# Graph attention kernel, first layer: wide matmuls for even blocks, h recomputed, x1 written late, adjacency stored in 8 KB pieces

## The reference, cut to what matters

```python
h = relu(layernorm(x))
# layer 0: attention
wh = h @ W;  e = wh @ a1 + (wh @ a2).T;  e = where(e > 0, e, 0.2 * e)
x1 = x + elu(softmax(where(adj > 0, e, -9e15)) @ wh)
# layer 1: cosine attention
h = relu(layernorm(x1))
Qn, Kn = cos_normalize(h @ Wq.T), cos_normalize(h @ Wk.T)
prop = softmax(where(adj > 0, Kn @ Qn.T, -9e15), axis=1) @ h
y = x1 + 0.5 * prop + 0.5 * h        # where a row has neighbours, else h
```

## Time and profile before

| | us |
|---|---|
| median of 3 runs (2190.71 to 2191.54) | 2190.98 |
| the profiled execution's own time | 2189.39 |
| its span, first to last instruction | 2187.6 |

### The profile page before, as it was taken

How to read it: one execution, slowest core, us unless ns; L and a number is a source line. 1 busy time by engine, 2 the same in 40 slices (tenths; PEclk the granted TensorE clock), 3 DMA queues, 4 the chain that set the end, 5 groups by cost and what they waited for, 6 DMA issues and landing times.

```text
span 2187.6 us, 63203 instructions
## 1 busy us (share of the span) xinstructions
PE 2142.1 (98%) x26185; PEld 1733.5 (79%) x26185; DVE 1963.5 (90%) x1686; ACT 1752.8 (80%) x1928; POOL 33.0 (2%) x43
## 2 busy tenths in 40 slices
PE   5999999999999979999999999999999999999998
PEld 5999999999999956777777777777777777777776
DVE  7999999999999858889888898898898898898987
ACT  6687778878788668888888888888888888888886
POOL 1000000000000030000000000000000000000000
PEclk9999999999999989999999999999999999999999
DMA  6899999999999916565565665665665666656653
GB/s 248 328 382 401 390 405 397 401 402 399 403 400 388 361 40 217 193 223 204 207 215 196 224 212 196 220 220 193 214 221 200 212 204 216 215 194 218 218 193 115
DMA packets 153732, 573.52 MB, mean 262 GB/s; under 512 B 9936, under 2 KB 10576, under 8 KB 153168
## 3 DMA queue, kind: packets, MB, share of 16 engines
q1 hardware_dynamic: 142176, 546.02, 68.3%
q10 hardware_dynamic: 11376, 24.91, 3.0%
HBM read 558.24 MB, written 12.65 MB: 261 GB/s over the span
## 4 chain that ended last, share of the span: by engine, by line
PE 95%; DVE 2%; ACT 1%; issue 1%; DMA 0%; POOL 0%; ACTq 0%; POOLq 0%; DVEq 0%
PE bank L1197 32%; PE bank L1245 30%; PE bank L1266 21%; PE bank L1261 10%; DVE hl_buf L726 1%; PE bank L1152 1%; PE bank L1172 0%; DVE hl_buf L714 0%; DMA ring<-adj 0%; ACT hl_buf L558 0%; ACT ring L619 0%; POOL hl_buf L401 0%; PE bank L1094 0%; PE bank L1134 0%; DMA q_buf<-x 0%
## 5 line engine op out<-in xcount | busy, mean ns | idle before, releaser
L619 ACT ACTIVATE ring<-bank,th_col 128x512 f32<-128x512 f32 x1024 | 647.1, 683 | 231.0 <-PE bank L1245 223.3
L988 DVE SCALAR_TENSOR_TENSOR ring<-ring 128x2048 f32<-128x2048 int32 x256 | 586.4, 2291 | 154.5 <-ACT ring L619 154.5
L1197 PE MATMUL bank<-v_buf,ring 128*128 128x129 f16 (+1 forms) x12288 | 711.9, 220 | 6.3 <-DVE ring L902 6.1
L1197 PEld LDWEIGHTS bank<-v_buf,ring 128*128 128x128 f16 x12288 | 707.8, 98 | 9.8 <-issue 8.9
L1245 PE MATMUL bank<-v_buf,q_buf 128*128 128x512 f16 x3072 | 706.4, 380 | 5.2 <-ACT ring L619 5.2
L1266 PE MATMUL bank<-u_buf,hl_buf 128*128 (+1 forms) x8192 | 704.3, 220 | 0.0
L1266 PEld LDWEIGHTS bank<-u_buf,hl_buf 128*128 128x128 f16 x8192 | 631.8, 98 | 55.9
L902 DVE SCALAR_TENSOR_TENSOR ring<-r_ring,th_word,ring 128x1024 f32<-128x1024 f32 x512 | 619.3, 1277 | 19.3 <-ACT ring L448 19.1
L993 DVE TENSOR_TENSOR hl_buf<-ring,hl_buf 128x2048 f16<-128x2048 f32 x256 | 584.5, 2284 | 0.0
L1261 PE MATMUL bank<-u_buf,hl_buf 128*128 (+1 forms) x2048 | 557.9, 272 | 0.5 <-DVE hl_buf L993 0.5
L448 ACT ACTIVATE ring<-ring 128x2048 f32<-128x2048 int32 x256 | 481.2, 1908 | 88.4 <-DMA ring<-adj 85.0
(11 more groups left out here) (138 smaller groups left out, 433.0 us busy)
## 6 DMA issues: line engine op xcount, KB each, us to landing
ring<-adj SPq DMA_DIRECT2D x512, 1024.0 KB, 5.6
r_ring<-a_rows SPq DMA_DIRECT2D x8, 512.0 KB, 7.0
x_dram<-q_buf ACTq DMA_DIRECT2D x8, 512.0 KB, 7.2
h_dram<-hl_buf ACTq DMA_DIRECT2D x8, 512.0 KB, 7.4
r_ring<-x_dram ACTq DMA_DIRECT2D x16, 256.0 KB, 4.2
r_ring<-h_dram ACTq DMA_DIRECT2D x16, 256.0 KB, 4.4
out<-r_ring ACTq DMA_DIRECT2D x16, 256.0 KB, 4.8
r_ring<-k_rows ACTq DMA_DIRECT2D x15, 256.0 KB, 4.1
```

Of the source, the lines that this page charges most:

```text
L619: ins = nc.scalar.activation(p_ring[:, k, (2 * hf + m) * IW:(2 * hf + m + 1) * IW], bank[:, 2 * hf + m, :], ACT.Exp, scale=q_scale[:, j:j ...
L988: V.scalar_tensor_tensor(p_ring[:, k, :], adj_ring[:, k, :], 0.0, p_ring[:, k, :], ALU.is_gt, ALU.mult).then_inc(s_m, 1)
L1197: ins = mm(acc0(par, it), weights0(k, ps)[:, it // 4, jj, f], v2[:, bass.ds((2 * j + us) * VW, D + 1)], start=False, stop=False, skip_grou ...
```

## The change

- **Even blocks of layer 0** take two matmuls instead of three: one of 259 columns (`WIDE`) over high and low values side by side, then low by high with 129. The slot has 40 matmuls instead of 48. The 8 sums take 4 banks a set instead of 3; the high-by-low sums of even blocks stand in columns of their own and are added on DVE: for the denominators by two copies, a sum and a reciprocal, for the features by four instructions in `negative` that add into `z_buf`.
- **The exponential** loses DVE's `min`. ACT now forms relu(-z) and then exp(-that), and `preset` (three instructions over 4 banks, 1552 elements a partition instead of 1032) moves from behind `quotient` to behind the exponential.
- **h**: the high part is written by ACT behind `normalised` instead of by DVE. h isn't written to DRAM; layer 1 forms it again from x1 in four ACT instructions a chunk (`residual_h`), for which `rstd` and `nbias` are kept for all tiles.
- **x1**: chunks 0, 4 and 7 are written by ACT as before, the others by SP behind the last loads of layer 0.
- **Banks**: the work between the layers uses other PSUM banks, and PE waits for the end of the added step ("low") of chunk 6 and chunk 7 where it waited for the quotient.
- `sizes` on ACT and its matmul move from chunk 1 to chunk 0.
- **Adjacency in DRAM**: for one load of layer 0 a partition's data is one piece of 8 KB; loads of layer 1 still take 4 KB pieces, now 8 KB apart.

```diff
 VW = D + 2
+WIDE = VW + D + 1
...
 EARLY = 4
+X1_EARLY = (0, 4, 7)
+X1_LATE = (1, 5, 2, 6, 3)
 FOLDS = (0, 16, 48, T)
 LN = ("diff", "total", "m2", "dsq", "between", "var", "rstd", "nbias")
-EPI0 = ("den", "neg", "elu", "x1", "stats") + LN + ("hi", "lo")
+EPI0 = ("densum", "den", "low", "elu", "x1", "stats") + LN + ("lo",)
...
         def acc0(par, it):
-            b, k = 3 * par + it // 3, it % 3
-            return bank[:, b, k * (D + 1):(k + 1) * (D + 1)]
-        def acc0_group(par, b):
-            n = min(3, IT0 - 3 * b)
-            return bank[:, 3 * par + b, 0:n * (D + 1)].rearrange("p (n c) -> p n c", n=n)
+            k = it % 2
+            return bank[:, 4 * par + it // 2, k * WIDE:k * WIDE + D + 1]
+        def acc0_wide(par, it):
+            return bank[:, 4 * par + it // 2, 0:WIDE]
+        def acc0_column(par, col):
+            return bank[:, 4 * par:4 * par + 4, col]
         def ht_bank(g):
-            return bank[:, 6 + g % 2, :].bitcast(F16)
+            return bank[:, 2 + g % 2, :].bitcast(F16)
         def qk_pair(g):
-            return 0 if g < EARLY else 2 * ((g - EARLY) % 2)
+            return 0 if g < EARLY else 4 * ((g - EARLY) % 2)
         def qk_banks(g):
             b = qk_pair(g)
             return bank[:, b:b + 2, :].rearrange("p b n -> p (b n)")
         def key_bank(i):
-            return bank[:, 4 if i == 0 else 6 if i == 1 else 4 + 2 * ((i - 1) % 2), :]
+            return bank[:, 7 if i == 0 else 6 if i == 1 else 4 + 2 * ((i - 1) % 2), :]
...
-            adj_lanes = adj.rearrange("b j p n -> p b j n")
+            adj_lanes = adj.rearrange("c j p b n -> p c j b n")
             def load0(c, j, k):
-                sp.dma_start(slot(k, I32).rearrange("p (b j n) -> p b j n", b=2, j=1),
-                             adj_lanes[:, bass.ds(2 * c, 2), bass.ds(j, 1), :]).then_inc(s_adj[k], 16)
+                sp.dma_start(slot(k, I32), adj[c, j].rearrange("p b n -> p (b n)")).then_inc(s_adj[k], 16)
             def load1(i, j, k):
-                sp.dma_start(adj_ring[:, k, :].rearrange("p (b j n) -> p b j n", b=1, j=2),
-                             adj_lanes[:, bass.ds(i, 1), bass.ds(2 * j, 2), :]).then_inc(s_adj[k], 16)
+                sp.dma_start(adj_ring[:, k, :].rearrange("p (j n) -> p j n", j=2),
+                             adj_lanes[:, i // 2, bass.ds(2 * j, 2), i % 2, :]).then_inc(s_adj[k], 16)
...
             chunks0(chunk)
+            for c in X1_LATE:
+                sp.wait_ge(s_ev, len(EPI0) * c + EPI0.index("x1") + 1)
+                sp.dma_start(x1_dram[:, c * C0:(c + 1) * C0], xs[:, c * C0:(c + 1) * C0]).then_inc(s_x1w[c % (NC0 // 2)], 16)
...
-                for i in range(3):
-                    g = acc0_group(par, i)
-                    ins = nc.scalar.activation(g, v_sum[:, :].unsqueeze(1).to_broadcast([P, g.shape[1], D + 1]),
+                sums = bank[:, 4 * par:4 * par + 4, 0:WIDE + D + 1]
+                nc.scalar.activation(sums[:, :, D + 1:WIDE].rearrange("p b (s n) -> p b s n", s=2),
+                                     ident[:, 0:D // 2 + 1].unsqueeze(1).unsqueeze(1).to_broadcast([P, 4, 2, D // 2 + 1]),
+                                     ACT.Copy, scale=0.0)
+                for k in range(2):
+                    ins = nc.scalar.activation(sums[:, :, k * WIDE:k * WIDE + D + 1],
+                                               v_sum[:, :].unsqueeze(1).to_broadcast([P, 4, D + 1]),
...
                     ins.then_inc(s_free, 1)
-                    if not (isinstance(c, int) and c == NC0 - 1):
-                        act.wait_ge(s_free, c + 1)
-                        act.nop(nofuse=True)
+                def exponential():
+                    act.wait_ge(s_ev, at("low"))
+                    nc.scalar.activation(e_buf, z_buf, ACT.Relu, scale=-1.0).then_inc(s_neg, 1)
+                    act.wait_ge(s_neg, c + 1)
+                    nc.scalar.activation(e_buf, e_buf, ACT.Exp, scale=-1.0).then_inc(s_ea, 1)
+                    if c != NC0 - 1:
                         preset(par)
-                def exponential():
-                    act.wait_ge(s_ev, at("neg"))
-                    nc.scalar.activation(e_buf, e_buf, ACT.Exp).then_inc(s_ea, 1)
                 def root():
-                    act.wait_ge(s_ev, at("x1"))
-                    act.dma_start(x1_dram[:, bass.ds(c * C0, C0)], xs[:, bass.ds(c * C0, C0)]).then_inc(s_x1w, 16)
+                    if c in X1_EARLY:
+                        act.wait_ge(s_ev, at("x1"))
+                        act.dma_start(x1_dram[:, bass.ds(c * C0, C0)], xs[:, bass.ds(c * C0, C0)]).then_inc(
+                            s_x1w[c % (NC0 // 2)], 16)
...
                         act.wait_ge(s_ev, at("nbias"))
-                        if not (isinstance(c, int) and c == 0):
-                            act.wait_ge(s_hw, 16 * c)
                     act.nop(nofuse=True)
                     for it in range(lo, hi):
                         ins = nc.scalar.activation(h_buf[:, it * P:(it + 1) * P], xs[:, bass.ds(c * C0 + it * P, P)],
-                                                   ACT.Relu, bias=nbias[:, it:it + 1], scale=rstd[:, it:it + 1])
+                                                   ACT.Relu, bias=nbias[:, c * IT0 + it:c * IT0 + it + 1],
+                                                   scale=rstd[:, c * IT0 + it:c * IT0 + it + 1])
                     if hi < IT0:
                         return
                     ins.then_inc(s_ea, 1)
                     act.wait_ge(s_ea, 3 * c + 3)
-                    act.dma_start(h_dram[:, bass.ds(c * C0, C0)], h_buf).then_inc(s_hw, 16)
+                    nc.scalar.activation(u_buf[:, bass.ds(c * IT0, IT0), 0:D], h_buf.rearrange("p (t f) -> p t f", f=D),
+                                         ACT.Copy).then_inc(s_uh, 1)
...
                     parts = {2 * (q - ZR) + 2: (lambda q=q: value_high(q)) for q in range(ZR, T // ZT)}
-                    parts[25] = lambda: preset(1)
+                    def second_set():
+                        act.wait_ge(s_wsum, 2)
+                        preset(1)
+                    parts[23] = sizes
+                    parts[25] = second_set
...
-            act.wait_ge(s_x1w, 16 * (NC0 - 1))
             def copy_ht(g):
+                act.wait_ge(s_x1w[g // 4], 32)
...
-            act.wait_ge(s_x1w, 16 * NC0)
-            act.wait_ge(s_hw, 16 * NC0)
...
                 act.dma_start(e_x1, x1_dram[:, bass.ds(i * IW, IW)]).then_inc(s_fin, 16)
-                act.dma_start(e_h, h_dram[:, bass.ds(i * IW, IW)]).then_inc(s_fin, 16)
+            def residual_h(i):
+                act.wait_ge(s_fin, 16 * (i + 1))
+                for it in range(IT1):
+                    f, t = slice(it * P, (it + 1) * P), i * IT1 + it
+                    ins = nc.scalar.activation(e_h[:, f], e_x1[:, f], ACT.Relu, bias=nbias[:, t:t + 1], scale=rstd[:, t:t + 1])
+                ins.then_inc(s_eh, 1)
             def chunk1(i, par):
                 first = isinstance(i, int) and i == 0
                 parts = {}
                 if not first:
                     quotient, store = epilogue1(i - 1, 1 - par)
-                    parts = {(0, 2): lambda: key_high(i + 1), (1, 1): quotient, (2, 1): store, (2, 2): lambda: residual(i),
+                    parts = {(0, 2): lambda: key_high(i + 1), (1, 1): quotient, (2, 1): store, (2, 2): lambda: residual(i), (3, 2): lambda: residual_h(i),
                              (2, 3): lambda: load_factors(i + 2)}
                     if i + 1 >= NI:
                         parts.pop((0, 2))
                     if i + 2 >= NI:
                         parts.pop((2, 3))
                 else:
-                    parts = {(0, 0): lambda: load_factors(1), (1, 2): lambda: key_high(1), (2, 1): lambda: load_factors(2)}
+                    parts = {(0, 0): lambda: load_factors(1), (1, 2): lambda: key_high(1), (2, 1): lambda: load_factors(2),
+                             (2, 2): lambda: residual_h(0)}
...
-            def scale_bias(lo, hi, at, done):
-                V.reciprocal(rstd[:, lo:hi], small[:, 4, lo:hi]).then_inc(done, 1)
+            def scale_bias(lo, hi, at, done, base=0):
+                to = slice(base + lo, base + hi)
+                V.reciprocal(rstd[:, to], small[:, 4, lo:hi]).then_inc(done, 1)
                 dve.wait_ge(done, at("rstd"))
-                V.scalar_tensor_tensor(nbias[:, lo:hi], small[:, 1, lo:hi], -0.5, rstd[:, lo:hi],
+                V.scalar_tensor_tensor(nbias[:, to], small[:, 1, lo:hi], -0.5, rstd[:, to],
...
                     dve.wait_ge(s_used, U0 * (c + 1))
-                    for b in range(3):
-                        g = acc0_group(par, b)
-                        ins = V.reciprocal(den[:, 0, 3 * b:3 * b + g.shape[1]], g[:, :, D])
-                    ins.then_inc(s_ev, 1)
+                    V.tensor_copy(den[:, 1, 1:IT0:2], acc0_column(par, WIDE + D))
```

(41 more changed lines are left out.)

15 lines of the change are left out of this document (7 added, 8 removed).

## The result

The changed kernel takes 2204.07 us (median of five runs, 2200.56 to 2208.91), the kernel before 2190.98 (2190.71 to 2191.57): 13.1 us more, a ratio of 1.006 with a 95% interval of 1.0049 to 1.0071. The forecast was +8.5. The profiled execution of the changed kernel took 2204.07 us, its span is 2202.20. The two traces differ by more than the medians, 14.65 us, mostly because the profiled execution of the kernel before (2189.39) was 1.6 us faster than its median.

What follows compares the result with a forecast made beforehand. DVE, not PE, was taken to set the pace of layer 0. Layer 0 +5.4, between the layers +2.5 and layer 1 +0.6 summed to +8.5 us on 2190.98, giving 2199.5 us, range 2184 to 2207.

Steps and rivals of the forecast that it cites:

- DVE sets the pace: Layer 0: DVE's path of 88.45 us a chunk exceeds PE's 86.6, so saved matmuls turn into PE waits.
- Part 1: PE in layer 0: a pair of blocks falls from 344.4 to 338 ns, the chunk to 86.6 us.
- rival A: Layer 0: PE's saving of 11.5 us arrives because DVE's path falls below 86.6 us; 2182.6 us, chance 0.15.
- Part 2: DVE's work in a layer 0 chunk: denominators +0.36, `negative` +0.42, `split` -0.72; sum +0.06, 84.8 us.
- Part 3: DVE's waits for ACT's masks: slot 10 from 1.30 to 2.2 us, slot 18 from 1.00 to 1.6, slot 6 gone.
- Part 4: Layer 0 summed over its chunks, five of them at 88.45 against 88.17 us: +5.4 us (-1 to +12).
- Rival C: ACT late as well: slot 10 costs up to 1 us more a chunk, fallen clock 2 more; 2207, chance 0.1.
- Part 5: DMA: larger load pieces taken at 0 (-2 to 0), late writes of x1 at 0.
- Part 6: Between the layers: later denominators, sums, Relu and high copy add 2.5 us (+1 to +5).
- The +0.6 for the high copy on ACT: Between the layers: ACT's copy of h's high part stands ahead of the squares whose sums release PE, +0.6 us.
- Part 7: Layer 1: `residual_h` is covered in the steps except at the end, +0.6 us (0 to 1).

Runs made afterwards that it cites:

- e6: Changed kernel with the next chunk's row factors (512 KB) loaded ahead of a chunk's last 8 slots instead of ahead of slot 8: 2199.79 us.
- e2: Changed kernel with layer 0's adjacency laid out and loaded as before, in 4 KB pieces: 2205.07 us.
- e8: Changed kernel with Exp's table load taken out of the loop ahead of slot 10 by a one-column Exp behind slot 7: 2196.05 us.
- e10: Changed kernel with only the order between the layers altered: ACT's copy 6 ahead of the exponential, DVE's residual ahead of its copy 7: 2203.62 us.
- e4: Changed kernel with h's high part copied by DVE again instead of ACT: 2203.77 us.

## Why the prediction was right in sign and short in size

The forecast said slower and named DVE's waits for ACT as the reason, and both hold. The size was 13.1 us for 8.5: 2204.07 is inside the stated range (2184 to 2207) and just above the band of 2195 to 2204 that had the 0.55.

**DVE sets the pace: right.** The chunks at the floor take 88.3 us (forecast 88.45). By DVE's starts of slot 0, chunk against chunk, the two kernels differ by +0.4, +0.8, +2.0, +2.7, -0.2, +1.6, +2.5 and +0.7 us for chunks 0 to 7, 10.5 in sum. Take out what chunks 3, 5 and 6 took above 88.3 (1.4, 1.6, 2.3) and 5.2 are left, where the forecast had 5.4. That the two agree so well is luck in part, since chunks 1 and 2 gave 2.8 for the 4.2 forecast and chunk 3 took the rest; the sum is nevertheless what was worked out.

**Part 1: a term mis-sized.** A pair of blocks takes 339.8 ns, not 338. The two columns more than in layer 1 are right (259 and four times 129 against 258, three times 129 and once 128), and 337 + 0.8 = 338 follows; layer 1's pairs are 337.5 ns apart in the trace. The other 1.5 ns of layer 0's pair have no cause that I can show. PE's pace is 87.0 us a chunk, and rival A would have been worth 8.5 us, not 11.5. Nothing of the result hangs on it, since PE waits. (By the Trainium skill, TensorE: Matmul & The Clock Gate, section Wait — 56ns, not 53.3ns?, a warm matmul takes N / 2.4 GHz + 2.5 ns, and a pair of 775 columns in five matmuls would be 335.4 ns, an estimate; the row gives 339.8, so this stream of small matmuls again has more overhead than the page.)

**Part 2: right.** (One reading in front of it is miswritten: the 9.65 us of the earlier trace rows are eight instructions, which are four slots and not eight; the 2.39 us a slot that the sum uses is right.) Denominators 0.57 (0.57 forecast), the four sums 1.04 (1.02), the `split` without its cast 560.15 - 559.02 = 1.13 for 1.87 before, -0.74 (-0.72).

**Part 3: right in all three waits, where ACT is early.** Slot 10: 2.17 us idle (2.2), slot 6: none, slot 18: 1.50 between the products, 1.6 with the hand-over (1.6). (88.6 less 0.1 is 88.5 and not the 88.45 of the sum, which changes nothing.) `preset` took 1.58 (1.7), and the table load 1.28 with Exp 0.01 behind it. The rows of slot 18, DVE and then ACT:

```profile
554.23 4.87 DVE L929 SCALAR_TENSOR_TENSOR ring<-r_ring,th_word,ring 128x1024 f32<-128x1024 f32 x4 [1.50 <-ACT ring L456]
```

```profile
548.04 3.19 ACT L527 ACTIVATE hl_buf<-q_buf,nbias,rstd 128x128 f32<-128x128 f32 x8 [2.53 <-DVE nbias L727]
551.27 1.06 ACT L534 ACTIVATE u_buf<-hl_buf 128x1024 f16<-128x1024 f32 x1
552.23 16.31 ACT L456 ACTIVATE ring<-ring 128x2048 f32<-128x2048 int32 x9
```

**Part 4: the step that failed.** "This holds if ACT is early; where it is late the wait is longer" was written, and then the sum took five chunks at 88.45 as if ACT were early in all. What the runs showed in its place: chunks 2 and 4 at 88.3 us, and chunks 3, 5 and 6 at 89.7, 89.8 and 90.6. The rows spoke against an ACT that is early: in chunk 5 of the kernel before ACT was late at slot 6 by 1.19 us, and by its trace the mask of slot 9 was ready only 0.2 to 1.1 us ahead of DVE in chunks 4 to 6. That lateness cost nothing then; the loads of slot 8 took 7.1 to 7.6 us in those chunks. In the change loads of 7.9 to 8.3 us delay the start of a loop of 8 us that ends at DVE, and the three chunks are 5.3 us above the floor: 4.7 ahead of slot 10, of which about 0.7 goes with the fall of the clock in chunk 5, 0.3 in the pause ahead of slot 4, and the rest in how the windows are cut. Rival C named this mechanism, with up to 1 us a chunk and a chance of 0.1: it was 1.4 to 1.9 us in three chunks of seven. e6 shows that the row factors' load is behind it in chunk 5 and behind most of it in chunk 6; for chunk 3 it stays open.

**Part 5: right.** The layout is worth 0 (e2), and the late writes of x1 delay nothing in layer 1 (1359.82 against 1359.90).

**Part 6: near at the clock of before, 4.0 for 2.5 in all.** 3.3 us had accrued when PE took up its matmuls behind the longest wait (30.76 against 27.49), and 0.7 lies between these matmuls and the first scores, 9.11 us against 8.39. In e8, with the same instructions and the lower clock for 10.2 us as in the kernel before, the passage took 38.65, 2.8 more than before. The other 1.2 stands beside a longer stretch at the lower clock (17.1 us), which the forecast had named and left for the range. e10, with copy 6 and `residual` no longer behind the Relu and the sums, is at 29.09 at the first mark and at 8.45 for the rest. The +0.6 for the high copy on ACT is not borne out by e4, where the copy is DVE's and the passage no shorter.

**Part 7.** +0.3 for +0.6, and no loss in the steps, as worked out.

So of the 6.15 us by which the profiled span exceeds the forecast, the late chunks are 5.3, the passage 1.5, and the small terms -0.6.

## What to carry to other kernels

Where two engines run within 2% of each other, price a change on the second engine's path first: the 1.2 us a chunk saved on PE was worth nothing until DVE's waits were short enough, and `preset`, 1.6 us long, cost up to 12 us inside the loop ahead of slot 10 against behind slot 20, where nothing waits for it. A step moved to another engine's queue costs about its length if it lands inside a loop that comes back to the pacing engine (1.6 us a chunk for `preset`, 1.1 for the table load of 1.28), so list each such loop from its first instruction to the one that waits for it, and put moved work outside all of them. And compute a loop twice, with its feeding engine early and with it as late as the trace shows it somewhere; a lateness that costs nothing today is the first thing that a tighter loop brings to light.

## What the runs showed of the hardware

**The granted clock fell after short waits in a busy stretch.** PE in chunk 5 of the change, then busy times in a stretch around it:

```profile
538.25 0.39 PE L1227 MATMUL bank<-v_buf,ring 128*128 x4
540.64 0.28 PE L1224 MATMUL bank<-v_buf,ring 128*128 x1 [2.00 <-DVE ring L929]
...
541.79 0.42 PE L1224 MATMUL bank<-v_buf,ring 128*128 x1
```

```profile
541.00:545.00 4.00, 4.00 (x39) 3.65 (x37) 4.00 (x4) 4.00 (x3) 0.00 (x0) 0.57 0.78 328
```

PE stood idle for 2.00 us ahead of slot 12; from 541.5 on, the clock was at its lower level of 1.2 GHz for 3.4 us, and a pair of blocks took 0.65 us for 0.34. In the twelve profiled executions there are 19 places in layer 0, after chunk 0, where two matmuls start 2.2 us or more apart; at 9 of them the clock fell within 1 us of the second start, and nowhere else in that stretch; 36 places with starts 1.0 to 2.1 us apart had no fall of their own. The kernel before has no such place. What a fall costs is not what PE loses in it (1.6 us), for PE had slack: chunk 5 took DVE 89.8 us with a fall (the change) and without one (e10). It comes back in the next chunk by way of loads that are issued up to 1.6 us later: slot 10 waited 4.1 us instead of 3.4 in chunk 6 (the change against e10), 4.0 instead of 3.6 in chunk 3, 4.3 instead of 2.3 in chunk 4 (e4, with its own edit in it), 2.4 instead of 2.3 in chunk 7. It may be why the five runs of the change spread over 8.4 us and those of before beside them over 0.9 (5.4 in a longer series of 22 runs), and the mean granted clock of the change's five, from the fastest to the slowest, is 0.993, 0.993, 0.991, 0.991 and 0.990; but only one execution of each kernel has a trace, so that is argued and not shown.

**Pieces of 8 KB and of 4 KB cost nearly the same per byte.** A packet of 8 KB took 309 ns in the change and one of 4 KB 159 ns in the kernel before, both as medians over the adjacency's loads.
